# A wait moved behind the eighth gather: the joints around the node stage of a two-layer graph network

## What is computed

```
x = layernorm(x + relu(segment_sum((x @ W0)[src] * norm) + b0))          # layer 0
x = layernorm(x + interaction(x, src, dst, edge data, weights))          # layer 1
# interaction, cut:
sj, vj = xs[idx_j], xv[idx_j]                   # rows of projected x1, gathered by dst
W      = (shifted_softplus(f_ij @ Wf1 + bf1) @ Wf2 + bf2) * rcut_ij      # a filter for each edge
x_ij   = products of sj, vj, Yv and W
agg    = segment_sum(x_ij, idx_i)               # summed by src
out    = per-node matmuls and a softplus of agg
```

## Time and profile before

| what | value |
|---|---|
| median of 3 runs | 1081.26 us (1080.84 to 1082.22) |
| profiled execution | 1074.51 us |
| its span | 1072.7 us |
| mean granted TensorE clock | 0.908 |
| first joint | 328 to 341 us of the span |
| second joint | 598 to 617 us of the span |

### The profile page before, as it was taken

One profiled execution on the slowest core, in us unless ns is written; L12 is line 12 of the kernel. 1 busy time (PEld: TensorE's weight loads), 2 busy tenths in 40 slices (PEclk: granted clock), 3 DMA queues, 4 the chain that ended last, 5 costly groups with the idle time before them and its releaser, 6 DMA issues.

```text
span 1072.7 us, 17283 instructions
## 1 busy us (share of the span) xinstructions
PE 920.3 (86%) x4812; PEld 743.0 (69%) x4812; DVE 846.7 (79%) x2396; ACT 707.3 (66%) x1642; POOL 652.9 (61%) x945
## 2 busy tenths in 40 slices
PE   7889888999973999999999389999999999915553
PEld 7767777777753888887888268888887888714443
DVE  7688888886824788788889578888888888719997
ACT  4669877777761566666666446666666666638886
POOL 4028888888851566666666345776677676426665
PEclk9989999998995999999999789999999999955555
DMA  9989999999998499999998767999999999688995
GB/s 350 418 274 250 242 237 240 239 240 242 236 224 279 165 341 324 327 315 313 323 323 311 273 187 178 216 206 218 226 217 211 216 228 189 94 220 337 389 400 233
DMA packets 121443, 280.39 MB, mean 261 GB/s; under 512 B 13746, under 2 KB 38342, under 8 KB 121350
## 3 DMA queue, kind: packets, MB, share of 16 engines
q1 hardware_dynamic: 73590, 186.25, 47.9%
q0 software_dynamic: 35280, 82.63, 40.0%
q10 hardware_dynamic: 12480, 10.42, 3.0%
HBM read 132.38 MB, written 146.87 MB: 260 GB/s over the span
## 4 chain that ended last, share of the span: by engine, by line
PE 43%; DVE 11%; DMA 8%; issue 4%; ACT 2%; POOL 1%; SPq 1%; ACTq 0%; DVEq 0%; POOLq 0%
PE bank L1309 8%; PE bank L1357 7%; PE bank L1340 6%; PE bank L1371 5%; DVE stat L1167 4%; PE bank L1313 4%; PE bank L1369 3%; DMA edge_mem<-x 3%; PE bank L1334 3%; PE bank L1300 2%; PE bank L1367 2%; DMA G_mem<-x 2%; PE bank L1346 2%; DVE node_mem L1158 1%; DVE stat L1043 1%
## 5 line engine op out<-in xcount | busy, mean ns | idle before, releaser
L548 POOL DMA_INDIRECT sum<-R_mem,sidx_all x79 | 129.1, 1634 | 85.0 <-DMA sum<-zeros 48.7
L609 POOL DMA_INDIRECT sum<-R_mem,l_sidx x79 | 135.6, 1717 | 45.9 <-issue 21.9
L595 POOL DMA_INDIRECT G_mem<-x_d,dst_i x79 | 77.2, 977 | 90.9 <-PE bank L1344 64.3
L1309 PE MATMUL bank<-G_hi 128*128 128x512 f32 x316 | 131.4, 416 | 0.0
L1309 PE MATMUL bank<-G_lo,G_hi 128*128 128x512 f32 x316 | 124.9, 395 | 0.0
L1225 PE MATMUL bank<-G_hi,M_mem 128*128 128x512 f32 x200 | 86.3, 432 | 7.0 <-ACT R_mem L681 6.4
L1313 PE MATMUL bank<-G_hi,G_lo 128*128 128x512 f32 x316 | 85.3, 392 | 0.0
L1114 DVE SCALAR_TENSOR_TENSOR edge_mem<-edge_mem,Y,bank 128x128 f32<-128x128 f32 x237 | 71.2, 385 | 15.0 <-ACT edge_mem L806 15.0
L1340 PE MATMUL bank<-edge_mem,Winv 128*128 128x512 f32 x158 | 81.8, 600 | 0.1
L1225 PE MATMUL bank<-G_lo,M_mem 128*128 128x512 f32 x200 | 80.5, 402 | 0.0
L1387 PE MATMUL bank<-ident,node_mem 128*128 128x128 f32 x80 | 27.5, 447 | 61.5 <-DVE node_mem L1158 61.5
(11 more groups left out here) (230 smaller groups left out, 2831.5 us busy)
## 6 DMA issues: line engine op xcount, KB each, us to landing
node_mem<-sum SPq DMA_DIRECT2D x41, 512.0 KB, 5.9
filt_d<-node_mem SPq DMA_DIRECT2D x40, 512.0 KB, 4.9
node_mem<-filt_d SPq DMA_DIRECT2D x79, 256.0 KB, 4.9
sum<-zeros SPq DMA_DIRECT2D x33, 512.0 KB, 14.2
G_mem<-x SPq DMA_DIRECT2D x20, 512.0 KB, 6.9
x_d<-node_mem SPq DMA_DIRECT2D x20, 512.0 KB, 3.5
edge_mem<-x SPq DMA_DIRECT2D x19, 512.0 KB, 6.1
x_d<-R_mem SPq DMA_DIRECT2D x19, 512.0 KB, 3.9
```

Of the source, the lines that this page charges most:

```text
L548: pool.indirect_dma_start(sum0, bass.IndirectOffsetOnAxis(ap=sidx[:, t:t + 1], axis=0), R[t % 8][:, :], None, compute_op=ALU.add).then_inc ...
L595: pool.indirect_dma_start(G3[t % 8][:, :], None, x1_d, bass.IndirectOffsetOnAxis(ap=dst_i[:, t:t + 1], axis=0)) \
L609: pool.indirect_dma_start(sum1, bass.IndirectOffsetOnAxis(ap=l1_sidx[0:n, t:t + 1], axis=0), R3[t % 8][0:n, :], None, compute_op=ALU.add). ...
L1309: pe.matmul(bank[4 + a][:, :], zT_hi[a][:, c * P:(c + 1) * P], w[c][:, :], start=(c == 0 and w is W0h), stop=False)
```

## The change

1. The helper `held` and its four semaphores go; its callers wait plainly.
2. On SP, the target blocks 0 to 3 and filter blocks 0 to 3 were issued at j = T2 + 1, ahead of the x1 stores of pairs 35 to 39. Now target block 0 and filter block 0 are issued behind the store of pair 37, and the other three of each behind all x1 stores.
3. The copies into sum1 of pairs 36 to 39 were issued behind their x1 stores (38 and 39 behind the last). Now they are issued when the eighth gather of the second edge stage has landed.
4. Row-tile 77 is normalised by VectorE instead of ACT, so n_last now counts to 2.
5. At the first joint TensorE waits for the last scatter of the first edge stage and then runs three matmuls of zeros, 128x512, into a bank that no one reads.

```diff
@@ SP
-                if j == T2 + 1:
-                    for g in range(4):
-                        trow_in(g)
-                    sp_.wait_ge(n_tr, TR)
-                    for t in range(4):
-                        filt_in(t)
                 if j >= 6:
                     i = j - 6
-                    sp_.wait_ge(n_x1, min(2 * i + 2, TR - 1))
-                    if i == T2 - 1:
-                        sp_.wait_ge(n_last, 1)
+                    sp_.wait_ge(n_x1, min(2 * i + 2, TR - 2))
+                    if i >= T2 - 2:
+                        sp_.wait_ge(n_last, i - T2 + 3)
                     sp_.dma_start(layer_pair(x1_d, i, 0, D), in_pair(res2[i % 8], i, 0, D)).then_inc(n_st[i % 8], 16)
-                    for k in ((i,) if i < T2 - 2 else (i - 1, i) if i == T2 - 1 else ()):
-                        sp_.dma_start(layer_pair(sum1, k, C, D), in_pair(res2[k % 8], k, C, D)).then_inc(rows_st[k % 8], 16)
+                    if i < T2 - 4:
+                        sum1_out(i)
+                    if i == T2 - 3:
+                        sp_.wait_ge(n_tr, TR)
+                        trow_in(0)
+                        filt_in(0)
+
+            def sum1_out(k):
+                sp_.dma_start(layer_pair(sum1, k, C, D), in_pair(res2[k % 8], k, C, D)).then_inc(rows_st[k % 8], 16)
 
             for j in range(T2 + 6):
                 nodes0(j)
+            for t in range(1, 4):
+                filt_in(t)
+                trow_in(t)
+            sp_.wait_ge(f_gather[7], 16)
+            for k in range(T2 - 4, T2):
+                sum1_out(k)
@@ POOL and ACT: four calls of this kind
-                    held(pool, n_rs, 2 * (g + 1))
+                    pool.wait_ge(n_rs, 2 * (g + 1))
@@ ACT
-                    if t8 < TR - 1:
+                    if t8 < TR - 2:
                         act.activation(r, r, ACT.Identity, bias=tiny[b][:, 6, k:k + 1], scale=tiny[b][:, 5, k:k + 1]).then_inc(n_x1, 1)
@@ ACT
-                    if t9 < TR - 1:
+                    if t9 < TR - 2:
                         act.wait_ge(n_x1, t9 + 1)
                     else:
-                        act.wait_ge(n_last, 1)
+                        act.wait_ge(n_last, t9 - TR + 3)
@@ DVE
-            dve.wait_ge(n_root, 2 * K_RSTD)
-            r = res[(TR - 1) % 16]
-            dve.tensor_scalar(r, r, w[:, 5, 0:1], w[:, 6, 0:1], ALU.mult, ALU.add).then_inc(n_last, 1)
+            for t in (TR - 2, TR - 1):
+                g, k, r = t // 2, t % 2, res[t % 16]
+                dve.wait_ge(n_root, K_RSTD * (g - T2 + 3))
+                dve.tensor_scalar(r, r, tiny[g % 4][:, 5, k:k + 1], tiny[g % 4][:, 6, k:k + 1], ALU.mult, ALU.add).then_inc(n_last, 1)
@@ PE
+            def keep_clock(b, n):
+                for _ in range(n):
+                    pe.matmul(bank[b][:, :], zeros[:, 0:P], zeros[:, 0:512], start=True, stop=True)
@@ PE
             ins.then_inc(s_pairs, 1)
+            pe.wait_ge(e_scat, 16 * TR)
+            keep_clock(7, 3)
```

More of the change, by code:

```diff
@@ L377, in build @@
         rows_st = [sem(f"rows_st{i}") for i in range(8)]
[L379 to L387, removed]
         NZ = 8
@@ L569, in nodes0 @@
                     st.mark(pool.tensor_tensor(w[:, 4, :], w[:, 3, :], w[:, 0, :], ALU.mult))
-                    held(pool, n_rstd, st.reached())
+                    pool.wait_ge(n_rstd, st.reached())
                     st.mark(pool.tensor_scalar(w[:, 3, :], w[:, 4, :], -0.5, 1.5, ALU.mult, ALU.add))
@@ L828, in edges1 @@
                     t, a = s - 2, (u - 2) % 8
-                    held(act, f_gather[a], 16 * (turn(t, a, 8) + 1))
+                    act.wait_ge(f_gather[a], 16 * (turn(t, a, 8) + 1))
                     wait(act, f_tr, t - 3)
```

## The result

| kernel | median | range | runs |
|---|---|---|---|
| before | 1081.36 us | 1080.84 to 1082.22 | 4 |
| changed | 1093.66 us | 1089.40 to 1095.86 | 4 |

The ratio is 1.0108, with a 95% interval of 1.0077 to 1.0140: the changed kernel is slower by 1.1%, 11.7 us by the ratio and 12.3 by the medians. The forecast was 1091.8 in 1087 to 1096.5, slower. The profiled execution of the changed kernel has a span of 1092.2 us, against 1072.7. That is 19.5 us, more than the runs show (the profiled execution of the kernel before took 1074.51 us, 6.85 less than its median), and the first thing to do is to see where it lies.

The account below looks back on a forecast made before the run. The prediction took chains of waits at two joints as bounding, though TensorE was busy 86%. +11.9 (second joint) - 1.4 (first) = +10.5 us on 1074.51 gives 1085.0, carried to the median 1091.8; range 1087 to 1096.5.

Parts of the forecast that it names:

- The deciding step: Second joint (node stage to second edge stage): ACT's first proj waits for four sum1 copies behind the eighth gather; +11.9 us.
- the head start: Second joint: the last x1 store lands at 609.0 instead of 611.76, 2.8 us sooner.
- The stores: Second joint: blocks and copies moved from ahead of the last x1 store clear its DMA backlog, which cost 2.7 us.
- They are hidden by the hold itself.: Second joint: filter and target blocks 1 to 3 may slow an early gather, 5.1 instead of 3.4 us, without delaying ACT.
- rival (c): Second joint, line 791: ACT's wait is over when the first gather lands; kernel 4.2 us faster, 1077.1; 3%.
- The first joint: First edge stage to node stage: matmuls of zeros raise TensorE's clock earlier; -1.4 us, ends -2.2 and +1.0.
- Rival (a): First edge stage to node stage: matmuls of zeros only delay, +1.0 in place of -1.4; total +12.9, 1094.2; 12%.
- the node stage keeps the gain: Node stage: TensorE hardly waits, 0.7 us from 347 to 600, so a start gained at its beginning is kept throughout.
- No step made up for the hold: Second edge stage: judges the rival that the fill with eight tiles at hand makes up the hold's cost, no change; 2%.
- The sum: Whole kernel: +11.9 - 1.4 = +10.5 us, carried to a median of 1091.8; 78%.

Follow-up runs that it names:

- The late hold: Changed kernel with ACT's wait for the last four sum1 copies moved from before its first proj to before its first write into R_mem; ratio to before 0.9990.
- the copies alone: Kernel before with only the sum1 copies of pairs 36 to 39 moved behind the eighth gather; ratio 1.0146, 15.7 us slower.
- the repeat: Changed kernel, unaltered, run again beside the kernel before on one chip; ratio 1.0092, 9.9 us slower.
- the warm matmuls alone: Kernel before with only the three matmuls of zeros after the last scatter of the first edge stage; ratio 0.9998.
- the blocks behind the second gather: Changed kernel with ACT's wait moved to its first write into R_mem, and filter and target blocks 1 to 3 issued after the second gather lands; ratio 0.9967.

## Why the prediction was right, point by point

**The deciding step** was ACT's wait at line 791, and it was right as put. The late hold takes the loss away by moving that wait alone, and the copies alone bring it back. Its terms, each from the changed kernel's chain, with the forecast in brackets: first gather to the issue of the eighth 8.92 (forecast 8.92); its landing 3.63 (3.6); first copy's issue to the last one's landing 635.91 - 630.51 = 5.40 (5.4); ACT's begin 0.19 behind (0.1); landing of the last x1 store to the first gather 0.82 (0.82). The store's landing was 3.47 where 3.0 was taken, so the head start was 2.3 and not 2.8. The joint came to +12.4 and +12.6 in two pairs of profiles, against +11.9.

**The stores.** The backlog was all but gone, as forecast. But the reason given, filter blocks and copies together, was wider than needed: the two copies alone did it.

**"They are hidden by the hold itself."** True of the changed kernel, and it hid a cost: with the hold gone, the blocks took 2.3 us from the first gather. So rival (c), 4.2 us faster if the wait did not bind, was wrong in its price. With the wait out of the way and nothing else changed the kernel was level with before; besides the gather, the 2.6 us of the steady part, whose cause is open, stand against it. With the blocks moved as well, and without that loss, it gained 3.5.

**The first joint.** Forecast -1.4, seen -1.8 and -1.5 in two pairs of profiles. The clock rose 4.7 and 5.1 us behind the first warm matmul in the two profiles of the changed kernel, where 5.65 was taken. Without warm matmuls it rose 5.65 and 5.5 us behind the first transposes in the two profiles of the kernel before, but 4.1 in the copies alone, whose program on TensorE is the same; that the two rises which the prediction went by lay within 0.1 us was chance. The Trainium skill ("TensorE: Matmul & The Clock Gate", Part 1) says that this point shifts from run to run, and these traces agree. Rival (a), that zeros would not raise the clock, is excluded: it rose before the first transposes. The premise that the node stage keeps the gain is not shown, as told above, since that stage differs by up to 4 us between executions.

**No step made up for the hold.** From the first proj to the end the two kernels differ by 0.6 us. That eight tiles stood ready bought nothing in the fill: the fifth proj falls 10.35 us behind the first in the changed kernel and 10.36 before.

**The sum** was +10.5. By ratio the runs gave +11.7 (interval 8.3 to 15.1) and, in the repeat, +9.9. The two pairs of profiles give, for the two joints, +10.6 and +11.1. That the sum is this close owes something to luck: the joint was 0.5 to 0.7 us longer than forecast and the first joint's gain up to 0.4 larger, which cancel in part, and the runs tell the total only to some 3 us.

## What to carry to other kernels

When a transfer is moved behind a later event, search every queue for waits on its semaphore and ask where each stands, not only who needs the data: here ACT needed the buffers ten steps later than it asked for them. A wait hoisted to the head of a stage costs nothing as long as its signal is early, and turns into the length of the moved chain when it is not. And what a hold hides comes out when the hold is removed, so a transfer issued beside the one on the critical path is to be priced once more after each repair. An engine made faster for a moment can also run into the next late transfer and lose its clock there, as TensorE did when the second joint was warmed.

## What was not expected

- The first edge stage, the same program in each kernel, was over at 334.8 to 337.6 us on two chips and at 342.9 to 344.2 on a third. The medians of the kernel before differ by 0.6% between these chips (1072.51 to 1078.90) and by 0.8% with the 1081.36 of the result, more than a part of a change like this is worth. Only runs on one chip were comparable.
- In the kernel with the late wait, the steady step of the second edge stage was 3.986 us in its profile (271.08 us over the 68 steps from the ninth proj), against 3.948 with the warm matmuls alone, 2.6 us in all (the kernel before had 3.954 in both of its profiles). The step of one product group shows it, first the late wait and then warm alone (timelines of TensorE):

```profile
756.79 0.40 PE L1360 MATMUL bank<-G_lo,M_mem 128*128 128x512 f32 x1
757.20 0.46 PE L1370 MATMUL bank<-MV,edge_mem 128*128 128x128 f32 x2
```

```profile
757.96 0.40 PE L1363 MATMUL bank<-G_lo,M_mem 128*128 128x512 f32 x1
758.21 0.46 PE L1373 MATMUL bank<-MV,edge_mem 128*128 128x128 f32 x2
```

  The next product begins 0.41 us behind instead of 0.25. The kernel with the blocks behind the second gather has the same program on ACT, VectorE and TensorE and a step of 3.955, so it isn't that program's alone. The cause stays open.
- A half-size copy took 10.52 us behind three others and among eight gathers and six blocks, and 3.50 us behind the same three with nothing else under way.
